# Two fused 32-head attentions: scores in 8 products instead of 12, and another order within a step

## What is computed

```python
q, k, v = x_n @ Wq, ctx @ Wk, ctx @ Wv          # layer 2 adds biases
q, k = rmsnorm(q) * wq, rmsnorm(k) * wk         # layer 1 alone
w = softmax(q @ k.T * 128**-0.5 + mask)         # the mask in layer 1 alone
x = x + (w @ v) @ Wo
```

## Time and profile before

| | |
|---|---|
| median of 3 runs | 1982.03 us (1981.51 to 1982.15) |
| the profiled execution | 1980.66 us, its span 1979.0 us |
| TensorE busy | 1777.9 us (90%) |
| DVE, ACT, POOL busy | 52%, 37%, 48% |
| the two attentions' steps | 406.6 to 1789 us of the span |
| mean granted TensorE clock | 0.93 of 2.4 GHz |

### The profile page before, as it was taken

How to read it: one execution, slowest core, us unless ns; L and a number is a source line. 1 busy time by engine, 2 the same in 40 slices (tenths; PEclk the granted TensorE clock), 3 DMA queues, 4 the chain that set the end, 5 groups by cost and what they waited for, 6 DMA issues and landing times. The chain is left out here.

```text
span 1979.0 us, 27876 instructions
## 1 busy us (share of the span) xinstructions
PE 1777.9 (90%) x9392; PEld 1493.6 (75%) x9392; DVE 1032.6 (52%) x2182; ACT 731.6 (37%) x2382; POOL 955.7 (48%) x977
## 2 busy tenths in 40 slices
PE   3799965689999999999999999999999999987666
PEld 2788854478888888888887888888888888875455
DVE  5466656434555555545564554455544444444554
ACT  2188820233333333333433433333433343441121
POOL 2033310165655767555566675555755665542002
PEclk9899987689999999999998999999999999998755
DMA  3000010121121222111111232122222222201011
GB/s 123 22 2 0 0 37 0 52 68 59 54 65 54 70 59 76 54 53 55 54 54 50 67 87 65 54 65 65 70 70 65 70 81 64 64 27 38 1 51 43
DMA packets 56928, 104.25 MB, mean 53 GB/s; under 512 B 7904, under 2 KB 8416, under 8 KB 56672
## 3 DMA queue, kind: packets, MB, share of 16 engines
q1 hardware_dynamic: 55072, 98.86, 16.9%
q10 hardware_dynamic: 1728, 3.75, 0.5%
HBM read 100.49 MB, written 2.10 MB: 52 GB/s over the span
## 5 line engine op out<-in xcount | busy, mean ns | idle before, releaser
L858 POOL TENSOR_TENSOR a_probs<-a_probs,a_total 128x512 f32<-128x512 f32 x128 | 133.4, 1042 | 407.8 <-DVE a_total L1269 407.8
L83 POOL TENSOR_TENSOR a_w_lo<-a_raw,a_w_hi 128x512 fp32r<-128x512 f32 x186 | 241.5, 1298 | 14.9
L68 PE MATMUL ps<-a_wo_hi,a_oT_lo 128*128 128x512 f32 x544 | 224.7, 413 | 8.8 <-DVE x L1291 4.7
L68 PE MATMUL ps<-a_xT_hi,a_w_lo 128*128 128x512 f32 x512 | 219.7, 429 | 4.9 <-DVE a_w_lo L83 4.8
L69 PE MATMUL ps<-a_wo_lo,a_oT_hi 128*128 128x512 f32 x544 | 213.5, 392 | 0.0
L70 PE MATMUL ps<-a_wo_hi,a_oT_hi 128*128 128x512 f32 x544 | 213.1, 392 | 0.0
L70 PE MATMUL ps<-a_xT_hi,a_w_hi 128*128 128x512 f32 x512 | 206.7, 404 | 0.0
L69 PE MATMUL ps<-a_xT_lo,a_w_hi 128*128 128x512 f32 x512 | 206.7, 404 | 0.0
L83 POOL TENSOR_TENSOR a_wo_lo<-a_raw,a_wo_hi 128x512 fp32r<-128x512 f32 x128 | 168.0, 1313 | 10.3
L83 DVE TENSOR_TENSOR a_pT_lo<-ps,a_pT_hi 128x512 fp32r<-128x512 f32 x192 | 128.8, 684 | 24.6 <-ACT a_pT_hi L1677 19.9
L69 PE MATMUL ps<-a_kT_lo,a_qT_hi 128*128 128x128 f32 x512 | 141.1, 276 | 0.0
(11 more groups left out here) (371 smaller groups left out, 4692.8 us busy)
## 6 DMA issues: line engine op xcount, KB each, us to landing
a_raw<-in_L_wq SPq DMA_DIRECT2D x128, 256.0 KB, 2.6
a_raw<-in_L_wo SPq DMA_DIRECT2D x128, 256.0 KB, 2.6
a_raw<-in_L_wkv SPq DMA_DIRECT2D x64, 256.0 KB, 2.6
x<-in_x ACTq DMA_DIRECT2D x8, 256.0 KB, 8.9
setup_raw<-in_cT SPq DMA_DIRECT2D x4, 512.0 KB, 7.1
a_raw<-in_L_main SPq DMA_DIRECT2D x8, 256.0 KB, 3.0
a_c_raw<-in_context SPq DMA_DIRECT2D x2, 1024.0 KB, 7.3
out<-x SPq DMA_DIRECT2D x8, 256.0 KB, 2.0
```

The source lines that it names most:

```text
L68: pe.matmul(out, lhs_lo, rhs_hi, start=start, stop=False)
L83: return eng.tensor_tensor(out_lo, value, hi.bitcast(F32), ALU.subtract)
L858: pool.tensor_tensor(heads(probs[:, :]), heads(probs[:, :]), along_last(total[:, :], S), ALU.mult).then_inc(s["probs"], 1)
```

## The change

The keys' two halves come to lie side by side in one tile, 128 high and 128 low columns for each item. A head's scores are then two products: the high half of the queries by both halves of the keys (256 columns), and the low half of the queries by the high half of the keys (128 columns, into the first 128 of the output). The scores take two banks; bank_out goes, and `project_out` writes into the bank of `mix`. ACT copies the second 128 columns of each head to SBUF (`take_cross`, new), DVE adds the first to them (`sum_scores`, new), and mask, maximum and exponentials read that sum in SBUF instead of PSUM. The order within a step changes on TensorE, ACT and DVE; POOL's and SP's lists stay. `add_out` comes a step earlier, `sums` a step later, and `mix` waits for `add_out` where `project_out` did.

```diff
-        kT, qT = [ph.split(f"kT{p}", UNIT * S) for p in (0, 1)], [ph.split(f"qT{p}", HQ * UNIT * S) for p in (0, 1)]
+        kT, qT = [ph.sb(f"kT{p}", 2 * UNIT * S, F32R) for p in (0, 1)], [ph.split(f"qT{p}", HQ * UNIT * S) for p in (0, 1)]
+        cross = ph.sb("cross", HQ * S)
-        bank_k, bank_q, bank_v, bank_s, bank_pT, bank_o, bank_out, bank_f = (C.ps[:, blk(k, BANK)] for k in range(8))
+        bank_k, bank_q, bank_v, bank_pT, bank_o, bank_f = (C.ps[:, blk(k, BANK)] for k in (0, 1, 2, 5, 6, 7))
+        bank_s = C.ps[:, 3 * BANK:5 * BANK]
+        bank_out = bank_o
...
@@ TensorE, scores(t) @@
-                if normed(t - 1):
-                    wait_from_one(pe, s["masked"], HQ * t)
-                else:
-                    pe.wait_ge(s["exped"], HQ * t)
+                wait_from_one(pe, s["sum"], t)
+                k_both = head(kT[u % 2], j, 2 * S)
                 for h in range(HQ):
-                    last = matmul_split(pe, head(bank_s, h), tuple(head(x, h * UNIT + j) for x in qT[u % 2]),
-                                        tuple(head(x, j) for x in kT[u % 2]), True, True)
+                    q_hi, q_lo = (head(x, h * UNIT + j) for x in qT[u % 2])
+                    out = head(bank_s, h, 2 * S)
+                    pe.matmul(out, q_hi, k_both, start=True, stop=False)
+                    last = pe.matmul(out[:, 0:S], q_lo, k_both[:, 0:S], start=False, stop=True)
@@ TensorE, the loop @@
-                if is_item(P):
-                    project(P)
                 if is_item(t + 1):
                     scores(t + 1)
                 if is_item(t):
                     turn(t)
+                if 0 <= P - 1 < LAYER_ITEMS:
+                    sums(P - 1, max(0, t + 1))
+                if is_item(t - 1):
+                    project_out(t - 1)
                 if is_item(t + 1):
                     values(t + 1)
-                if is_item(t - 1):
-                    project_out(t - 1)
+                if is_item(P):
+                    project(P)
                 for h in (0, 1):
                     ffn(h, t - F_STEP[h])
                 if is_item(P) and P % HQ == HQ - 1:
                     project_values(P // HQ)
                 if is_item(t):
                     mix(t)
-                if is_item(P) and normed(P):
-                    sums(P, max(0, t + 2))
@@ ACT @@
+            def take_cross(t):
+                act.wait_ge(s["s_mm"], t + 1)
...
+                act.activation(heads(cross[:, :]), score_parts()[1], ACT.Copy).then_inc(s["cross"], 1)
@@ DVE @@
+            def sum_scores(t):
+                dve.wait_ge(s["s_mm"], t + 1)
+                dve.wait_ge(s["cross"], t + 1)
+                dve.tensor_tensor(heads(cross[:, :]), score_parts()[0], heads(cross[:, :]), ALU.add).then_inc(s["sum"], 1)
```

More of the change, by code:

```diff
@@ L764, in heads, with parts, score_parts, by_item @@
             return tile.rearrange("p (h c) -> p h c", h=HQ)
+        def parts(tile):
+            both = tile[:, :].rearrange("p (j c t) -> p c j t", c=2, t=S)
+            return both[:, 0], both[:, 1]
+        def score_parts():
+            both = bank_s.rearrange("p (h c t) -> p c h t", c=2, t=S)
+            return both[:, 0], both[:, 1]
+        def by_item(v):
+            return v.rearrange("p (j t) -> p j t", t=S)
         def normed(t):
@@ L1075, in keys @@
                     g = group_of(u)
-                    act.activation(kT[u % 2][0][:, :], bank_k, ACT.Identity, bias=bk_cols[:, g:g + 1]).then_inc(s["k_hi"], 1)
+                    act.activation(parts(kT[u % 2])[0], by_item(bank_k), ACT.Identity, bias=bk_cols[:, g:g + 1]).then_inc(s["k_hi"], 1)
             def split_keys(u):
@@ L1080, in split_keys @@
                 wait_from_one(act, s["s_mm"], UNIT * (u - 1))
-                act.activation(kT[u % 2][0][:, :], kn[:, :], ACT.Copy).then_inc(s["k_hi"], 1)
+                act.activation(parts(kT[u % 2])[0], by_item(kn[:, :]), ACT.Copy).then_inc(s["k_hi"], 1)
             def queries(P):
@@ L1100, in exps @@
                     act.wait_ge(s["pT_mm"], t)
[L1101 removed]
+                src = probs if normed(t) else cross
                 for h in range(HQ):
@@ L1154, in _ @@
                     split_oT(t - 1)
+                if is_item(t + 1):
+                    take_cross(t + 1)
+                if is_item(t):
+                    split_pT(t)
                 for h in (0, 1):
                     ffn(h, t - F_STEP[h])
[L1157 to L1169, removed]
+                if is_item(P) and P % HQ == 2 and normed(P):
+                    split_keys(P // HQ)
                 if is_item(t + 1):
@@ L1172, in _ @@
                     exps(t + 1)
+                if is_item(P):
+                    u, h = P // HQ, P % HQ
+                    queries(P)
+                    if h == 0:
+                        keys(u)
         @block.vector
@@ L1394, in _ @@
             dve.wait_ge(s["weight"], 1)
-            for t in range(-LOOK, ITEMS + 2):
+            for t in range(-LOOK, ITEMS + 1):
                 P = t + LOOK
@@ L1401, in _ @@
                     split_oT(t - 1)
-                if is_item(t - 2):
-                    add_out(t - 2)
+                if is_item(t + 1):
+                    sum_scores(t + 1)
+                if is_item(t):
+                    split_pT(t)
+                if 0 < P <= ITEMS and P % HQ == 0:
+                    take_values(P // HQ - 1)
                 if 0 <= P - 1 < LAYER_ITEMS:
@@ L1407, in _ @@
                     query_scales(P - 1)
-                if 0 < P <= ITEMS and P % HQ == 0:
-                    take_values(P // HQ - 1)
-                for h in (0, 1):
-                    ffn(h, t - F_STEP[h])
-                if is_item(P):
-                    u, h = P // HQ, P % HQ
-                    if h == 2 and normed(P):
-                        scale_keys(u)
-                        split_keys(u)
-                    queries(P)
-                    if h == 0:
-                        keys(u)
-                if 0 <= P - 1 < LAYER_ITEMS and (P - 1) % HQ == 0:
-                    spread_key_scales((P - 1) // HQ)
+                if is_item(P) and P % HQ == 2 and normed(P):
+                    scale_keys(P // HQ)
                 if is_item(t + 1):
@@ L1425, in _ @@
                     maximum(t + 1)
-                if is_item(t):
-                    split_pT(t)
+                if is_item(P) and P % HQ == 2 and normed(P):
+                    split_keys(P // HQ)
+                for h in (0, 1):
+                    ffn(h, t - F_STEP[h])
                 if is_item(t + 1):
                     split_v(t + 1)
+                if is_item(t - 1):
+                    add_out(t - 1)
+                if 0 <= P - 1 < LAYER_ITEMS and (P - 1) % HQ == 0:
+                    spread_key_scales((P - 1) // HQ)
+                if is_item(t + 1):
+                    invert(t + 1)
                 for h in (0, 1):
@@ L1432, in _ @@
                     next_spread(h, t + 1 - F_STEP[h])
-                if is_item(t + 1):
-                    invert(t + 1)
+                if is_item(P):
+                    u, h = P // HQ, P % HQ
+                    queries(P)
+                    if h == 0:
+                        keys(u)
 HD0 = 16
```

26 lines of the change are left out of this document (15 added, 11 removed).

## The result

The changed kernel takes 2000.83 us in the median of four runs (1994.23 to 2001.15), the kernel before 1981.8. The ratio is 1.0088, with a 95% interval of 1.0067 to 1.0109 (the two medians alone would give 1.0096). It is slower, by 19 us in the medians. The profiled execution is the quickest of the four, 1994.23 us with a span of 1992.5, and it is compared with the profiled execution of before, whose span was 1979.0. The difference of the spans is 13.5 us.

A forecast was written before the change was run, and what follows sets the result against it. TensorE's instruction list was taken to bound the kernel. Layer 1 at -36 and layer 2 at +46 made +10 on the profiled execution's 1980.66: 1991 us, range 1950 to 2035.

The forecast's parts named there:

- Part 1: Score products on TensorE: eight instead of twelve save 0.38 us a step, -23 us in layer 1, -24 in layer 2.
- Part 2: New take_cross on ACT and sum_scores on DVE: some 0.6 and 0.7 us, costing nothing on TensorE in layer 2.
- Part 3: Layer 1: TensorE's wait for a_pT_lo goes, and a low-clock stretch with it; -28 us, between -15 and -33.
- Part 4: Layer 2: project_out, now close behind mix, waits for a_oT_lo; a stall of 0.47 us in each step.
- Part 5: Values behind project_out delay exponentials, normalise and Wo's chunks: 2.0 us a unit in layer 2; +16 us in layer 1, less 4.
- Part 6: New TensorE pauses lower the clock in a third of layer 2's 16 units: +9 us, between 0 and +50.
- The port: Masks with two SBUF inputs, delayed beside POOL in layer 1: up to 1.1 us a step covered, costed at nothing.
- Rival C: Layer 1 masks alternate with POOL's cast and subtraction, 0.9 us a step reaching TensorE: 2039 us; chance 0.13.
- a mean above 1 us: Sign on DVE: masks averaging more than 1 us would show the prediction wrong; 0.34 to 0.5 us expected.
- the routing: Layer 1: routing work on DVE delays the halves of oT; plus 3 us.

The follow-up runs named there:

- run 8: Run 6 with layer 2 alone reordered: project and values ahead of project_out, whose output goes to the bank of the turned probabilities; 1891.85 us, ratio 0.9567.
- run 4: Changed kernel with each head's scores again in three products of 128 columns, the rest of the new order kept; 2015.87 us, ratio 1.0174.
- run 6: Both repairs: the changed kernel with the edits of run 1 and run 5 together; 1927.05 us, ratio 0.9741.
- run 5: Changed kernel, but in layer 1 DVE writes the sum of the score halves back to PSUM, where the masks read it; 1965.5 us, ratio 0.9936.
- run 1: Changed kernel, but project_out of a unit's first item waits for each chunk of Wo just ahead of its own products; 1953.92 us, ratio 0.9863.

## Why the prediction was right, and where it was not

The prediction was slower, 1991 us in a range of 1950 to 2035, and 2000.83 was measured. The sign and the mechanism were right; one term was missing, and others made up for part of it. By its steps:

**Part 1, the scores.** Predicted 0.91 us for eight products, measured 0.85. A pair starts every 0.22 to 0.23 us (1501.73, 1501.96), as the 0.12 + 0.11 of the forecast had it, where the three products took 0.33. The two terms are not right one by one: 0.17 us pass behind the product of 256 columns and 0.06 behind that of 128 (1501.73, 1501.90, 1501.96), and only the sum came out. What was mis-sized is the first pair, which the next follows after 0.17 us (1501.56, 1501.73); I had taken 0.01 off for it. So 0.44 us a step and not 0.38. Where nothing waits behind it the gain is whole: layer 2 of run 8 is 27.7 us under the kernel before, a unit 38.21 - 36.23 = 1.98 us under, four steps of 0.44 and 0.05 more that I don't attribute. In the changed kernel's own order layer 1 keeps 16 us of it and layer 2 nothing (run 4).

**Part 2** stood where it was put, and no wait for its work is among TensorE's in layer 2; no run leaves it out. The sum ran at 1503.31 and a_pT_lo was done 3.04 us into the step, against the 3.2 predicted.

**Part 3.** The wait for a_pT_lo is gone. With both repairs layer 1 is 57.2 us under the kernel before; parts 1 and 3 had 51. No run separates the two exactly. The clock had more of it than the 5 us of part 3: it was low for 34 us of layer 1 in the kernel before and for 7 in run 6, 27 us less. Eight falls of 1.5 us each (run 5) are as long, so some 12 of the 57 are the clock, an estimate. The units of layer 1, 43.4 in the forecast, take 43.11 and, with a fall of the clock, 44.6.

**Part 4.** Predicted 0.47 us a step in layer 2. The products' waits show 0.3 each (12.7 us in 44), the weight loads' of the same stretch 0.6:

```profile
PEld ps L68 <- DVE a_oT_lo L1312: 27.0, 46, 2.6
```

The lengths of the units lie between: from runs 1 and 6 to run 8, where project stands ahead of project_out, the steady unit falls from 38.27 to 36.23, which is 0.51 us a step. Run 8 differs from them in more than this (the values, take_values, the bank), so the 0.51 is for all of it together.

**Part 5.** Predicted: a step of 8.17, normalise 7.0 into it, the second chunk done at 11.9, a pause of about 2.4, of which 2.0 were this part. Measured, in the step at 1483.16: 8.16, 6.97, 11.84 and a pause of 2.35. Run 1 takes the wait away and a unit falls by 2.07. The unit of layer 2 was to be "about 40.5 us" and is 40.34. In layer 1 the same wait was dearer in the forecast than on the chip: 16 - 4 = 12 us against the 7 between runs 5 and 6.

**Part 6, the clock.** Windows of 10 us around two like pauses of layer 2 answer to the earlier trace rows:

```profile
1532.00:1542.00 10.00, 7.65 (x32) 6.11 (x32) 4.68 (x8) 3.42 (x12) 6.84 (x8) 0.83 0.40 106
1491.00:1501.00 10.00, 7.65 (x41) 6.29 (x40) 4.98 (x9) 4.09 (x13) 8.16 (x10) 1.00 0.40 106
```

Both hold a pause of 2.35 us. In the first the clock was 0.83 in the mean, so a third of it passed at the lower level (1.2 GHz); in the second it stayed at the upper one throughout. A unit with such a fall takes 41.7 to 41.95 us instead of 40.34, 1.4 more (1.7 predicted, for which I had given no row), and three of the last eight units have one; in the whole stretch of layer 2 the clock fell eight times (a third of 16 predicted, so five). So at most 8 x 1.4 = +11 against +9; in the sum below it stands inside the 35 us of run 1. What decides whether a pause lowers the clock stays open.

**The port, costed at nothing.** This is the step that failed. The sentence was that "delays of the masks up to 1.1 us together are covered, four of 1.14 are not", and I took the median of the earlier trace rows, 0.36 us, as the ordinary case. Over all masks the delay is 0.24 us in the mean (580 ns against 342), less than I allowed; but in the steps where POOL splits chunks beside them four masks lose 2.6 us together (4.00 - 4 x 0.34), beyond what is covered: in 16 of 64 steps they lose more than 2 us, and in most of the others next to nothing. My own numbers did not bear the zero out either. Four delays of the median, 0.36 us, make 1.44, which is 0.34 more than the 1.1 that I held to be covered, and over 60 steps that is 20 us: near the 21 measured, by another distribution. The rule that I had weighed, in the Trainium skill, "SBUF — State Buffer", section "SBUF: two separate sides", says that the two engines lock each other out for a whole instruction: the timeline at 575.90 agrees for DVE, each mask being as long as POOL's instruction beside it (0.62 by a cast of 0.61, 1.46 by a subtraction of 1.30). It does not for POOL, which in those rows lost 0.07 us at most to masks that take 0.34 alone, nor for POOL's powers on 4 columns, which held up no mask (last section). The delay costs 21 us in layer 1, with its clock, and 6 in the unit after it. Rival C had the mechanism right and its price too high (48 more): not every step has chunks beside its masks, and it took each step to lose 0.9. I should have counted in how many steps POOL's chunks fall beside the masks. I had named a mean above 1 us as the sign of a wrong prediction; the mean was the wrong thing to watch, since more than half of the masks are not delayed at all.

**The sum, redone with what was measured.** Layer 1: -57 for parts 1 and 3, +7 for the wait for Wo (run 6 against run 5; 12 predicted), +21 for the masks: -29. Layer 2: -28 for the products, +33 for project_out close behind mix (run 6 against run 8; 30 predicted; in run 6 mix also waits 6.4 us there for add_out, which I had put at nothing), +35 for the wait for Wo with its clock (run 1; 32 - 5 + 9 predicted), +4 for the masks in the unit between the layers (run 6 against run 1): +44, or 44.8 before rounding. With -2.3 at the start and the rest +0.4 that is +13.5. So the missing term of 25 us was offset but for 4: the products and the gone wait brought 9 more than I took in layer 1 (51 less 3 for the routing) and 8 more in layer 2 (20), and the wait for Wo in layer 1 cost 5 less. That these met the missing term was luck, not working. The profiled execution was, besides, the quickest of its four; the median is 6.6 us above it.

## What to carry to other kernels

When an instruction is moved in one engine's list, follow the chain to the next thing that the same engine needs, through every other engine's list, and add up its offsets: here a transpose that holds TensorE for 0.03 us, moved behind 2.8 us of products, delayed exponentials, normalising and a weight split in turn, and with a wait for all four chunks at once it cost 35 us. A wait for the last of several pieces ahead of the first use is a hidden deadline; a wait for each ahead of its own use cost nothing and turned the loss of 19 us into a gain of 25. And before an intermediate moves from PSUM to SBUF, count how often the other engine on SBUF works beside its readers.

## What the runs showed of the hardware that I had not expected

- POOL's powers (-1/2, for the norms) on 4 columns, 1.01 us each (the first row of the timeline at 574.80), did not delay the masks beside them: the 85 masks that had only such an instruction beside them lasted 344 ns in the mean. Those beside the subtraction of a chunk of Wo alone lasted 1.45 us (14 of them), those beside a cast and a subtraction of a_w (the weights of queries, keys and values) 0.74 (27). The delay goes by the instruction beside the mask, not by POOL being busy.
- The pair of a 256-column and a 128-column product costs as much as one product of 512 columns (0.23 us), though it has 384.
- The same pause of 2.35 us lowered the clock in three of the last eight units and not in the others, with the same work around it. Executions of the changed kernel differ by up to 10 us (1990.88 to 2001.15); the quicker one of the first four had a mean clock of 0.928 and the others 0.925, so I put the spread down to such falls, which no run shows by itself.
